# Output projection one batch ahead: the second batch's tiles among the last attention steps, and three places for x

## What is computed

```
h  = x @ W.T + b + 2 * (x @ A[a]) @ B[a]             # low-rank adapter chosen per batch
o  = softmax(q k.T / sqrt(32)) v                      # 32 heads, 8 kv heads, q, k, v from h
x2 = x + o @ w_o
c  = x2 @ weight[id].T                                # 1024x1024 weight chosen per batch
out = x2 + sum_e gate_e(c) * (c @ A_e.T) @ B_e.T * 4  # top 2 of 4 experts, rank 16
```

## Time and profile before

| quantity | value |
|---|---|
| median of 3 runs | 1071.86 us (1070.69 to 1072.41) |
| the profiled execution | 1075.97 us, of which the span is 1074.3 us |
| PE busy | 1018.2 us (95%) |
| DVE, ACT, POOL busy | 635.1, 450.3, 233.7 us |
| mean granted TensorE clock | 0.978 of full |
| DMA | 117.41 MB, mean 109 GB/s |

### The profile page before, as it was taken

One profiled execution on the slowest core, in us unless ns is written; L12 is line 12 of the kernel. 1 busy time (PEld: TensorE's weight loads), 2 busy tenths in 40 slices (PEclk: granted clock), 3 DMA queues, 4 the chain that ended last, 5 costly groups with the idle time before them and its releaser, 6 DMA issues.

```text
span 1074.3 us, 17421 instructions
## 1 busy us (share of the span) xinstructions
PE 1018.2 (95%) x6934; PEld 822.1 (77%) x6934; DVE 635.1 (59%) x1071; ACT 450.3 (42%) x782; POOL 233.7 (22%) x224
## 2 busy tenths in 40 slices
PE   7999999999899998999989999899799999999997
PEld 6878787877578775777767787577488898898896
DVE  6562734567755578654776557664555655655653
ACT  5121223355544466543664556544523323323320
POOL 1000001133223333223331236443200100100100
PEclk9999999999899998999998999899989999999998
DMA  7030312011421124211132125435757667667531
GB/s 257 0 99 18 111 55 72 22 36 37 116 57 37 35 53 115 58 34 31 45 97 71 44 81 153 115 115 175 225 165 233 210 189 230 213 184 231 196 118 40
DMA packets 49888, 117.41 MB, mean 109 GB/s; under 512 B 7298, under 2 KB 26114, under 8 KB 45712
## 3 DMA queue, kind: packets, MB, share of 16 engines
q1 hardware_dynamic: 40080, 81.70, 26.0%
q0 software_dynamic: 9728, 34.61, 10.1%
HBM read 86.38 MB, written 18.89 MB: 98 GB/s over the span
## 4 chain that ended last, share of the span: by engine, by line
PE 83%; DVE 6%; ACT 4%; DMA 4%; POOL 1%; SPq 1%; issue 1%; ACTq 0%
PE psP L752 17%; PE psW L1038 16%; PE psF L254 11%; PE psG L1066 8%; PE psO L820 5%; PE psT L807 4%; PE psS L796 4%; PE psP L767 3%; PE psX L1281 3%; PE psO L824 3%; DVE q_stack L652 2%; PE psY L1300 2%; ACT probs L599 2%; ACT q_stack L565 1%; PE psF L265 1%; PE psM L831 1%
## 5 line engine op out<-in xcount | busy, mean ns | idle before, releaser
L672 DVE TENSOR_REDUCE nmax<-psS 128x2 f32<-128x512 f32 x256 | 164.7, 685 | 178.5 <-PE psS L796 176.8
L549 POOL TENSOR_TENSOR p_sum<-probs 128x512 f32<-128x512 f32 x128 | 167.1, 1305 | 395.3 <-ACT probs L599 395.1
L752 PE MATMUL psP<-x_hl,wq 128*128 128x512 f32 x960 | 238.1, 393 | 3.7 <-DVE q_stack L652 3.7
L752 PEld LDWEIGHTS psP<-x_hl,wq 128*128 128x128 f32 x960 | 174.8, 189 | 35.7 <-issue 4.4
L1038 PE MATMUL psW<-wq 128*128 128x256 f32 x1536 | 197.4, 284 | 1.6 <-DVE q_stack L652 1.1
L1038 PEld LDWEIGHTS psW<-wq 128*128 128x128 f32 x1536 | 191.1, 191 | 6.3 <-issue 1.5
L599 ACT ACTIVATE probs<-psT 128x512 f32<-128x512 f32 x256 | 139.1, 595 | 46.9 <-PE psT L807 45.8
L1047 ACT ACTIVATE cond_hi<-cond_raw 128x1024 fp32r<-128x1024 f32 x64 | 66.8, 1057 | 154.3 <-PE psG L1066 149.9
L1051 DVE TENSOR_TENSOR cond_lo<-cond_raw,cond_hi 128x1024 fp32r<-128x1024 f32 x64 | 78.3, 1235 | 89.7 <-ACT cond_hi L1047 89.6
L614 ACT ACTIVATE nmax_rows<-psM 16x128 f32<-16x128 f32 x64 | 17.1, 268 | 190.5 <-PE psM L831 190.5
L652 DVE TENSOR_TENSOR q_stack<-psP,q_stack 32x512 fp32r<-32x512 f32 x128 | 87.8, 686 | 8.0 <-ACT q_stack L565 5.9
(11 more groups left out here) (122 smaller groups left out, 1261.8 us busy)
## 6 DMA issues: line engine op xcount, KB each, us to landing
cond_raw<-in_cond POOLq DMA_DIRECT2D x64, 512.0 KB, 4.0
x_raw<-in_xT SPq DMA_DIRECT2D x32, 256.0 KB, 4.0
q_stack<-q_stack SPq DMA_DIRECT2D x32, 256.0 KB, 3.1
o_scratch<-o_sb SPq DMA_DIRECT2D x64, 128.0 KB
o_raw<-rden_scratch SPq DMA_DIRECT2D x32, 256.0 KB, 5.3
o_raw<-o_scratch SPq DMA_DIRECT2D x8, 1024.0 KB, 9.4
x_sb<-in_xT SPq DMA_DIRECT2D x8, 1024.0 KB, 6.8
outT<-x_sb SPq DMA_DIRECT2D x32, 256.0 KB, 2.5
```

The lines of the kernel that those rows point to most:

```text
L549: pool.tensor_tensor(p_sum[:, heads], probs[:, 0, heads], probs[:, 1, heads], ALU.add).then_inc(sum_done, 1)
L672: dve.tensor_reduce(nmax[:, n % 2, 2 * hp:2 * hp + 2, qt], psS[:, i % 2].rearrange("p (h k) -> p h k", h=2), AX.X, ALU.max, negate=True).t ...
L752: mm = pe.matmul(out, wq[:, i, w, k * P:(k + 1) * P], x[:, k, part], start=(k == 0 and n_ == 0), stop=False)
```

## The change

- The eight W_o tiles of batch 1 move ahead of their batch: tiles 0 to 4 stand at (16, 1) to (18, 1), each in front of the row of the conditioned weight there, and tiles 5, 6, 7 in PE's `first()`. In every later batch, PE makes the W_o tiles of batch n+1 beside the rows of batch n.
- So x needs three places: `x_sb[n % 3]`, the third where k of the attention lies. Its load (`load_x(2)`) waits for the end of attention.
- The loads and splits of o move too: `load_o(1)` and `load_x(1)` go from s = 13 to s = 12, ahead of the load of `RA`; `normalise(1)` stands at s = 13, `scale_hi(1)` at s = 14 (ahead of the split of `RA`), `scale_lo(1)` at s = 15. Batch 2 follows: `load_o(2)` at s = 17, and its normalise and split in `first()`.
- The last two batches have only eight W_o tiles left between them. `two()` spreads the 16 rows of batches 6 and 7 over those: two rows behind each of tiles 0 to 3, none behind tile 4, three behind tile 5, five behind tile 6. The turn of the gated values of batch 7 and its first two y tiles stand right behind those five rows.

```diff
+    TWO_AT = [[0, 1], [2, 3], [4, 5], [6, 7], [], [8, 9, 10], [11, 12, 13, 14, 15], []]
+    TWO_SPLIT = [[2, 3], [4, 5], [6, 7], [], [8, 9], [10, 11, 12], [13, 14, 15], []]
-    FIRST_TILES = {(12 + (m + 1) // 2, (m + 1) % 2): m for m in range(KT)}
+    AHEAD = 5
+    FIRST_TILES = {(12 + (m + 1) // 2, (m + 1) % 2): divmod(m, KT) for m in range(KT + AHEAD)}
-    x_sb = at("x_sb", [P, 2, KT, T], F32, R0 + 8192)
+    x_sb = [at(f"x_sb{i}", [P, KT, T], F32, offset) for i, offset in enumerate((R0 + 8192, R0 + 16384, R2))]
...
         if s == 12:
             sp.wait_ge(before.proj_done, PAIRS * NS)
+            load_o(sp, 1)
+            load_x(sp, 1)
             sp.dma_start(ra_raw[:], RA).then_inc(const_landed, 16)
-        if s == 13:
-            load_x(sp, 1)
-            load_o(sp, 1)
+        if s == 17:
+            load_o(sp, 2)
...
         sp.wait_ge(before.o_copied, N)
+        load_x(sp, 2)
...
     def w_o_tile(pe, n, m, ks):
         if ks[0] == 0:
+            if m == 0:
+                pe.wait_ge(o_lo_done, n + 1)
...
-        if s == 10:
-            scale_hi(act, 0)
+        if s in (10, 14):
+            scale_hi(act, (s - 10) // 4)
...
-        if part == 1 and s == 9:
-            normalise(dve, 0)
-        if part == 1 and s == 11:
-            scale_lo(dve, 0)
-        m = FIRST_TILES.get((s, 0) if part else (s - 1, 1))
-        if m is not None:
-            residual(dve, 0, m)
+        if part == 1 and s in (9, 13):
+            normalise(dve, (s - 9) // 4)
+        if part == 1 and s in (11, 15):
+            scale_lo(dve, (s - 11) // 4)
+        tile = FIRST_TILES.get((s, 0) if part else (s - 1, 1))
+        if tile is not None:
+            residual(dve, *tile)
...
         def first():                       # PE
-            for k in (5, 6, 7):
+            w_o_tile(pe, 1, 5, range(KT))
+            cond_row(pe, 0, 5)
+            w_o_tile(pe, 1, 6, range(KT))
+            for k in (6, 7):
                 cond_row(pe, 0, k)
-            pe.wait_ge(o_lo_done, 2)
-            w_o_tile(pe, 1, 0, range(KT))
+            w_o_tile(pe, 1, 7, range(4))
             turn_g(0)
+            w_o_tile(pe, 1, 7, range(4, KT))
             middle(0)
...
+        def two():                         # PE
+            n = B - 2
+            for m in range(KT):
+                w_o_tile(pe, n + 1, m, range(4))
+                if m == 4:
+                    turn_g(n)
+                if m == 7:
+                    y_tile(n + 1, 2)
+                    y_tile(n + 1, 3)
+                    turn_g(n + 1)
+                w_o_tile(pe, n + 1, m, range(4, KT))
+                if m == 4:
+                    middle(n)
+                for r in TWO_AT[m]:
+                    cond_row(pe, n + r // KT, r % KT)
+                if m == 1:
+                    turn_gated(n)
+                if m in (2, 3):
+                    y_tile(n, 2 * (m - 2))
+                    y_tile(n, 2 * (m - 2) + 1)
+                if m == 6:
+                    turn_gated(n + 1)
+                    y_tile(n + 1, 0)
+                    y_tile(n + 1, 1)
+            middle(n + 1)
```

More of the change, by code:

```diff
@@ L908, in finish_stage @@
     const_landed, fb_landed = sem("const_landed"), sem("fb_landed")
-    o_landed, x_landed = ([sem(f"{v}_landed_{c}") for c in range(2)] for v in "ox")
+    o_landed, x_landed = ([sem(f"{v}_landed_{c}") for c in range(slots)] for v, slots in (("o", 2), ("x", 3)))
     o_normal, o_hi_done, o_lo_done = sem("o_normal"), sem("o_hi_done"), sem("o_lo_done")
@@ L980, in sync @@
         for n in range(B):
-            if 2 <= n + 1 < B:
-                load_o(sp, n + 1)
             if n == 0:
                 before.store_rden(sp, PAIRS - 1)
[L985 to L989, removed]
+                continue
+            if n + 2 < B:
+                load_o(sp, n + 2)
+            store(n - 1)
+            if n + 2 < B:
+                sp.wait_ge(stored, 16 * YT * n)
+                load_x(sp, n + 2)
         store(B - 1)
@@ L1018, in residual @@
     def residual(dve, n, m):
[L1019 removed]
+        x2 = x_sb[n % 3][:, m]
         if m == 0:
[L1021 removed]
+            dve.wait_ge(x_landed[n % 3], 16 * (n // 3 + 1))
         dve.wait_ge(wo_done, KT * n + m + 1)
[L1023 removed]
+        dve.tensor_tensor(x2, x2, psW[:, m % 2, 0:T], ALU.add).then_inc(x2_done, 1)
     def w_o_tile(pe, n, m, ks):
@@ L1110, in ahead_tensor @@
     def ahead_tensor(pe, n, part):
-        m = FIRST_TILES.get((n - LAST, part))
-        if m is not None:
-            w_o_tile(pe, 0, m, range(KT))
+        tile = FIRST_TILES.get((n - LAST, part))
+        if tile is not None:
+            w_o_tile(pe, *tile, range(KT))
         k = ROWS_MULT.get((n - LAST, part))
@@ L1128, in gated_part, with copy_g, first, batch @@
             nc.scalar.activation(gated_hi[:], psX[:, 1, 0:T], ACT.Copy, scale=FFN_SCALE).then_inc(gated_hi_done, 1)
[L1130 to L1142, removed]
+        def copy_g(n):
             act.wait_ge(cond_used, KT * (n + 1))
             nc.scalar.activation(g_sb[:], psG[0:EC].rearrange("p a b -> p (a b)"), ACT.Copy).then_inc(g_copied, 1)
-            if n + 1 < B:
-                cond_row(KT * (n + 1))
-                cond_row(KT * (n + 1) + 1)
+        def first():
+            for k in (6, 7):
+                cond_row(k)
+            scale_hi(act, 2)
+            act.wait_ge(fb_landed, 32)
+            nc.scalar.activation(fb_stack[:], fb_raw[:], ACT.Copy).then_inc(fb_hi_done, 1)
+            copy_g(0)
+            for k in (0, 1):
+                cond_row(KT + k)
+        def batch(n):
+            gates(n)
+            for k in (2, 3):
+                cond_row(KT * n + k)
+            gated_part(n)
+            for k in (4, 5, 6, 7):
+                cond_row(KT * n + k)
+            if n + 2 < B:
+                scale_hi(act, n + 2)
+            copy_g(n)
+            for k in (0, 1):
+                cond_row(KT * (n + 1) + k)
+        def last():
+            n = B - 1
+            gates(n)
+            for k in (2, 3, 4, 5, 6, 7):
+                cond_row(KT * n + k)
+            gated_part(n)
+            copy_g(n)
         act.wait_ge(before.pv_done, N)
         act.wait_ge(before.o_copied, N)
-        for n in range(B):
+        first()
+        for n in range(1, B - 1):
             batch(n)
+        last()
         gates(B)
@@ L1209, in add_y, with first @@
         def add_y(n, j):
-            c = (n - 1) % 2
+            out = x_sb[(n - 1) % 3][:, 2 * j:2 * j + 2]
             dve.wait_ge(y_done, YT * (n - 1) + j + 1)
-            dve.tensor_tensor(x_sb[:, c, 2 * j:2 * j + 2], x_sb[:, c, 2 * j:2 * j + 2],
-                              psY[:, j % 2].rearrange("p (m t) -> p m t", m=2), ALU.add).then_inc(y_added, 1)
+            dve.tensor_tensor(out, out, psY[:, j % 2].rearrange("p (m t) -> p m t", m=2), ALU.add).then_inc(y_added, 1)
+        def first():
+            for e in range(E):
+                ins = dve.memset(chosen[:, e:e + 1], e - 1.5)
+            for i in range(E - 1):
+                dve.memset(later[:, i, 0:i + 1], 0.0)
+                ins = dve.memset(later[:, i, i + 1:E], 1.0)
+            ins.then_inc(chain, 1)
+            residual(dve, 1, 4)
+            cond_row(6)
+            normalise(dve, 2)
+            residual(dve, 1, 5)
+            cond_row(7)
+            dve.wait_ge(fb_hi_done, 1)
+            dve.tensor_tensor(fb_stack[ER:P], fb_raw[ER:P], f(fb_stack[ER:P]), ALU.subtract).then_inc(fb_lo_done, 1)
+            residual(dve, 1, 6)
+            turn_copies(0)
+            residual(dve, 1, 7)
+            scale_lo(dve, 2)
+            before.invert(dve, PAIRS - 1)
+            for k in (0, 1):
+                cond_row(KT + k)
@@ L1216, in batch @@
         def batch(n):
-            if n:
-                gates(n)
+            gates(n)
             for m in range(KT):
-                if m == 7 and n:
+                if m == 7:
                     turn_copies(n)
-                if n:
-                    residual(dve, n, m)
-                if m < 6 and (n or m >= 4):
+                residual(dve, n + 1, m)
+                if m < 6:
                     cond_row(KT * n + m + 2)
-                if m == 7 and n == 0:
-                    turn_copies(n)
[L1228 to L1256, removed]
+                if m == 1:
+                    gated_part(n)
+                if m in (2, 3):
+                    add_y(n, 2 * (m - 2))
+                    add_y(n, 2 * (m - 2) + 1)
+                if m == 3 and n + 2 < B:
+                    normalise(dve, n + 2)
+                if m == 6 and n + 2 < B:
+                    scale_lo(dve, n + 2)
+            for k in (0, 1):
+                cond_row(KT * (n + 1) + k)
@@ new lines, in two @@
+        def two():
+            n = B - 2
+            gates(n)
+            for m in range(KT):
+                if m == 4:
+                    turn_copies(n)
+                if m == 7:
+                    for j in range(YT):
```

(63 more changed lines are left out.)

7 lines of the change are left out of this document (3 added, 4 removed).

## The result

| | median, us | runs |
|---|---|---|
| before | 1072.72 | 7 (1070.69 to 1078.18) |
| changed | 1082.66 | 7 (1081.55 to 1084.75) |

The ratio is 1.0089, 95% interval 1.0068 to 1.0109: the change costs some 9.5 us (9.9 by the medians). The profiled execution took 1083.42 us, with a span of 1081.7. The prediction had the sign, but 1075.8 us is too little, and the measured time is outside its range of 1066 to 1081 us.

The account below looks back on a forecast made before the run. PE bound the kernel, with only its idle and low-clock time around the end of attention winnable: -13.2 us taken away, +13.7 idle added, +3.4 clock, sum +3.9 on 1071.9, so 1075.8 us; range 1066.0 to 1081.0.

Parts of the forecast that it names:

- the two falls of the clock: Around the end of attention, 757 to 762 and 775 to 785 us: both go, saving 1.7 + 3.4 = 5.1 us.
- the 7.7 us of waits: PE's waits between 753 and 776 us for low parts, g and split o: filled by batch 1's tiles, 7.7 us saved.
- the wait for the rows of maxima: PE's wait at 736.7 us: goes since the large loads start a step earlier, 0.4 us saved.
- Place A: Step 13, tile (0, 3): PE waits for a residual queued behind normalise(1), which waits for o; 3.3 us added.
- Place B: Step 15, tile (0, 7): PE waits for a residual behind scale_lo(1); 1.5 us added, bounds 0.9 to 2.5.
- Place C: Rows of steps 17 and 18: waits of 0.55 us for row 3 and 3.3 us at tile (1, 4) added.
- Place D: two(), last two batches: waits at rows 10, 13, 15 and the first y product of batch 7; 5.05 us added.
- The clock: Behind the new gaps at Place A and Place C: one short fall each, +3.4 us, and none in two().
- Steady batches and tail at nothing: Steady batches and the tail behind the last middle: same instructions and order of waits, covered by PE, no cost.
- Rival 1: Transfers quick, shrinking Place A, Place C and row 15's wait: -7.1 us, 1068.7 us; chance 0.29, with smaller two() cost.
- Rival 2: The clock stays full through the new gaps: 1072.4 us, no change; chance 0.19.
- Rival 3: Long clock falls at Place A, Place C and the end of two(), 3 x 3.4 us: 1082.6 us; chance 0.16.

Follow-up runs that it names:

- e8: The kernel before, unchanged, profiled a second time: span 1070.4 us, time 1072.15 us.
- e11: The kernel before, unchanged, profiled a third time: span 1071.2 us, time 1072.91 us.
- e1: Changed kernel with VectorE's residual put ahead of normalise(1) at step 13 and scale_lo(1) at step 15: 1076.38 us, ratio 1.0021.
- e7: Changed kernel with only the load of x of batch 1 moved from step 12 to step 13: 1082.3 us, ratio 1.0076.
- e2: Changed kernel with only the load of o of batch 2 moved from step 17 to step 16: 1079.73 us, ratio 1.0056.
- e3: Changed kernel with only the splits of row 4 moved from step 17 to step 18: 1077.6 us, ratio 1.0034.
- e4: Changed kernel with the last two batches' rows evened, two behind each of tiles 0 to 5, four behind tile 6: 1080.38 us, ratio 1.006.
- e5: Changed kernel with the edits of e1, e2, e3 and e4 together: 1066.21 us, ratio 0.9936.
- e9: Kernel of e5 with batch 7's gated values turned ahead of the last four rows, and normalise(0) moved from step 9 to 10: 1064.94 us, ratio 0.9923.

## Why the prediction was right in sign and wrong in size

The stretch that the change touches runs from the start of tile (0, 0) to the start of the last middle product. It took 350.2 us in the first profile of before (707.98 to 1058.18), 347.4 in e8 and 347.3 in e11, and 356.9 and 356.8 in the two profiles of the changed kernel. Against the first profile, on which the sum was made, that is +6.7 us where +3.9 was forecast; against the other two +9.5, which is what the medians show.

- **"With them go the two falls of the clock, 1.7 + 3.4 = 5.1 us" failed**, and it is the largest single error. The second fall cost 3.4 us in the first profile, nothing in e8 and 1.7 us in e11. The other terms held: the 7.7 us of waits are in the first profile and e8 (7.2 in e11), the 1.7 us of the first fall in all three, and the wait for the rows of maxima was 0.3, 1.0 and 0 us. The gain is thus 10.4 us against e8 and 10.6 against e11, not 13.2. Carrying a difference from an execution 3 us above its median to the median kept the error in.
- **Place A**, the tile (0, 3): the mechanism was right (e1), the size 4.3 instead of 3.3 us, since the load took 10.8 us and not the 9.8 of its twin. The prediction took it that x and RA, behind o in the same queue, cost it nothing. e7 moved x away and gained nothing, but RA and then x were still in flight before o was there, so why the load is slower stays open.
- **Place B**: 1.5 forecast, 1.25 measured; e1 removed it.
- **Place C**: row 3 as forecast (0.55, measured 0.52). Tile (1, 4): 3.3 forecast, 4.63 measured, because the row landed 6.1 us after its issue and I allowed 4.5. e2 shows that the load of o of batch 2 was the reason: I had named it and priced it at 0.45 us, and it was 2.1. This is the second term that failed. e3 shows that the tile waited for the residual alone.
- **Place D**: 5.05 forecast, 3.7 for rows plus 0.93 for the y product measured; in e4, with the rows evened, two of the three row waits went. Row 15 waited 1.56 us, not 1.75.
- **The clock**: a fall at A and one at C came in both profiles. I had taken two short ones, 3.4 us. Tile (0, 3) took 4.63 instead of 3.04 us and tile (1, 4) 5.44 instead of 3.04, 4.0 us together; the second fall was a long one. No fall came in `two()` in either. That they come was forecast; their cost was 0.6 us more.
- **Steady batches and tail at nothing**: right, PE is gapless from 801 us to the rows of `two()`.

Added in the profile are 10.2 + 0.5 + 3.7 + 0.9 = 15.3 us of idle and 4.0 us of clock, 19.3 against the 17.1 forecast; taken away are 13.2 in the first profile. That leaves 6.1 of the 6.7 us; against e8 and e11 it leaves 8.9 and 8.7 of the 9.5. The rest may be the longer first products behind each wait; it was not tested. Of the 5.6 us between the 3.9 forecast and the 9.5 measured, 2.8 are thus what the first profile had paid and e8 and e11 had not, 2.2 are terms of the added time that were too small, and 0.6 are open. The forecast of 1075.8 us missed by another 0.9 us in its base: three runs of the kernel before gave a median of 1071.86, seven gave 1072.72. Of the 7.4 us between the first two spans, 0.9 had come up before tile (0, 0), whose start lay between 707.0 and 708.9 us in profiles of both kernels.

Rival 1 (quick transfers) fell: transfers were slower. Rival 2 (clock full) fell. Rival 3 (long falls everywhere) has almost the measured time, 1082.6 us, but by luck: there was one long fall, not three. e5 checks the account from the other side. Its forecast was 16.6 us less than the changed kernel, and 16.5 came (16.4 by the ratios). Against the kernel before it gained 6.9 us (4.4 to 9.3): 10.5 less the 2.5 us of waits that it still has makes 8.0 and fits, 13.2 less 2.5 makes 10.7 and does not.

## What to carry to other kernels

When small work that a busy engine needs is queued behind an operation that waits for a transfer, that transfer holds the busy engine up; put the small work first (e1). It does not help where the small work is itself a transfer behind a large one (e9). Fill an idle stretch only after asking which transfers move with it: here a row's fetch, moved later by the tiles, fell into the next large load, which had itself been moved earlier. Before a low clock is booked as a gain, look at a second profile of the same kernel, since the fall behind scattered short waits was long in one execution here, short in another and absent in a third, while those behind the single waits of 3.4 us (kernel before) and of 4.3 to 4.9 us (changed kernel) came in every profile.

## What the runs showed of the hardware that was not expected

- A 512 KB fetch issued 4.5 us behind the start of a 2 MB load took 6.1 us to land, against 4.0 us with that load out of the way. The 2 MB load had begun on another queue.
- Of two loads with the same shape on the same queue, the one with only small transfers behind it took 9.7 to 10.2 us until VectorE could start, and the one with RA and x (1.3 MB) behind it 10.6 to 11.6, in every profile where VectorE stood for it. That these are the reason is not shown.
- The rows of maxima, 4 KB each, issued right behind the 2 MB load of o of batch 0, let TensorE go 7.7 us later (e9), and TensorE stood 2.0 to 2.6 us for them in every profile.
- The same kernel's middle product took 5.12, 3.79 and 3.79 us in three profiles, with a granted clock of 0.79 and 0.53 around the first and of 1.00 around the others.
